# A two-layer attention and mixture-of-experts kernel on one core: where the second expert matrices of the first layer come from

## The chip, the cores and the metric

The kernel runs on one NeuronCore of a Trainium2 chip. The time is the device time of one execution in microseconds (us); the value given for a kernel is the median of several executions. The engines are PE (TensorE: matmul, and PEld for its weight loads), DVE (VectorE), ACT (ScalarE), POOL (GpSimd) and SP (SyncE, which here only issues DMAs). Each has its own instruction sequencer, written PEldq, SPq, ACTq and DVEq in the rows: the sequencer does the register and branch instructions and hands the rest on to its engine.

## What is computed

The program is two transformer layers on x of 8 x 256 x 256 floats (2048 tokens of width 256). Each layer is a cross attention with 16 heads and then a mixture of experts. The change is in the expert part of the first layer:

```python
logits = jnp.einsum('sbd,de->sbe', x, Wg) + bg + bias
vals, idx = jax.lax.top_k(logits, 2)
w = jax.nn.softmax(vals - jnp.max(vals, axis=-1, keepdims=True), axis=-1)
cw = jnp.einsum('sbk,sbke->sbe', w, jax.nn.one_hot(idx, 16, dtype=x.dtype))
h = jax.nn.relu(jnp.einsum('sbd,edh->esbh', x, W1) + b1[:, None, None, :])
y = jnp.einsum('esbh,ehd->esbd', h, W2) + b2[:, None, None, :]
out = jnp.einsum('esbd,sbe->sbd', y, cw)
```

There are 16 experts; W1 of one is 256 x 512 and W2 of one is 512 x 256, 512 KB each in float32. Only the two chosen experts of a token are computed. x is added to the result, and the second layer (attention on the same context, then 7 experts with a capacity and one shared expert) follows.

## The kernel before

The program is a row of blocks that each end with a barrier of all engines: attention 0, `route_block` (layer 0), `experts0_block`, attention 1, `route_block` (layer 1), `experts1_block`.

**Routing.** `route_block` makes normalized rows `hall`, which SP stores to the DRAM tensor `rows` in eight DMAs (L1260), and from them the logits, the two picks of each token, and `block_expert`: the (token, expert) pairs are sorted by expert and cut into NB0 = 47 blocks of 128 rows, each of one expert. In this block SP also loads b1 and b2 of all experts (L1256, L1257) and, behind the row stores, ten DMAs of what attention 1 needs (`ahead`: four matrices of 256 KB, two bias vectors, two broadcast rows, two parts of the context; L1264 to L1270). Then it waits until the rows are stored.

**Experts.** `experts0_block` runs over the 47 blocks: block 0 is begun ahead, a hardware loop (Fori) of ROUNDS = 11 rounds handles RING = 4 blocks in each, and LEFT = 3 blocks follow it unrolled. For block n:

- SP reads the expert's number from `block_expert` into a register (L1573), waits until the second matmuls of block n-4 are done (`y_made`), and loads W1 and W2 of that expert, 1024 KB, into one of four ring buffers `w` (L1575).
- POOL gathers the 128 rows of x by an indirect DMA (L1589).
- PE transposes x (`turn`, L1703), DVE copies the transpose to SBUF (L1668), PE does the first matmuls (`first`, L1713: 8 of them, 16 in the trace, each of 128 columns), ACT adds the bias and applies relu (L1608), PE does the second matmuls (`second`, L1722: 4, in the trace 8, of 256 columns) and DVE adds b2 (L1676), ACT stores 128 KB of result (L1616).

PE's order is first(n+1), turn(n+2), second(n). first(n+1) waits for `w_loaded` of its ring buffer and for the transposed x of block n+1 (`xT_ready`). second(n) waits for ACT's `hid_ready`. ACT and DVE already read the expert's number into a register for each block, to address b1 and b2 (L1603, L1672). PE addresses only fixed places.

Of the kernel before, what the change touches and what calls it, by code (L numbers as in the profile page):

```python
# [50 lines left out]
W0 = DC * F0 + FC0 * D  # L51
NB0 = (2 * T + E0 * (P - 1)) // P
ROWS0 = NB0 * P

# [1125 lines left out]
def route_block(nc, m, layer, E, a, hall, router, shared=None, biases=None, rows=None, W=None, ctxT=None, ahead=None):  # L1180
# [7 lines left out]
    with ctx:  # L1188
# [64 lines left out]
        def _(sp):  # L1253
            if biases:
                b1, b2, b_loaded = biases
                sp.dma_start(b1[:], a["b1"]).then_inc(b_loaded, 16)  # L1256
                sp.dma_start(b2[:].rearrange("p e d -> p (e d)"), a["b2"].rearrange("e d -> (e d)").partition_broadcast(P)).then_inc(b_loaded, 16)  # L1257
                for n in range(B):
                    sp.wait_ge(h_ready, n + 1)
                    sp.dma_start(rows[n * S:(n + 1) * S, :].rearrange("(t p) d -> p t d", p=P),  # L1260
                                 hall[:, n * TPB:(n + 1) * TPB]).then_inc(rows_stored, 16)
                loaded = ahead["loaded"]
                for name in ("Wk", "Wv", "Wq", "Wo"):
                    sp.dma_start(ahead[name.lower()][:], W[name].rearrange("(c p) n -> p c n", p=P)).then_inc(loaded, 16)  # L1264
                for w, name in enumerate(("bq", "bk")):
                    sp.dma_start(ahead["bias"][:, w], W[name].rearrange("(c p) -> p c", p=P), allow_slow_non_contiguous=True).then_inc(loaded, 16)
                for name in ("bo", "bv"):
                    sp.dma_start(ahead["bo" if name == "bo" else "bvb"][:], W[name].partition_broadcast(P)).then_inc(loaded, 16)
                for j in range(2):
                    sp.dma_start(ahead["cst"][:, j], ctxT.rearrange("(c p) t -> p c t", p=P)[:, :, j * S:(j + 1) * S]).then_inc(loaded, 16)  # L1270
                sp.wait_ge(rows_stored, 16 * B)
# [241 lines left out]
def experts0_block(nc, m, a, rows, ye, b1, b2, b_loaded):  # L1513

    ctx = ExitStack()
    with ctx:
# [48 lines left out]
        def w2(j, f):  # L1565
            return w[:, j, DC * F0 + f * D:DC * F0 + (f + 1) * D]

        @block.sync
        def _(sp):
            def load(i, j):  # L1570
# [4 lines left out]
                sp.dma_start(w[:, j], a["W_0"][bass.ds(e, 1)].rearrange("a p f -> p (a f)")).then_inc(w_loaded[j], 16)  # L1575

            with sp.Fori(0, ROUNDS) as i:
                for j in range(RING):
                    load(i, j)
            for j in range(LEFT):  # L1580
                load(ROUNDS, j)
# [110 lines left out]
        def _(pe):  # L1692
# [23 lines left out]
            def second(i, j):  # L1716
# [4 lines left out]
                for f in range(FC0):  # L1721
                    last = pe.matmul(ps[:, YB + j % 2, 0:D], hid[:, j % 2, f, :], w2(j, f), start=f == 0, stop=f == FC0 - 1)  # L1722
                last.then_inc(y_made, 1)

            def round_of(i, known):

                for j in range(min(known, RING)):
                    if j + 1 < known:
# [3 lines left out]
                    second(i, j)  # L1732
# [10 lines left out]
            first(0, 0)  # L1743
            with pe.Fori(0, ROUNDS) as i:
# [431 lines left out]
def two_layers(nc, a, out):  # L2176

    with ExitStack() as ctx:
# [17 lines left out]
        with ExitStack() as layer, signals(nc, m["resting"]) as signal:  # L2196
# [7 lines left out]
            with ExitStack() as experts, signals(nc, m["resting"]) as signal:  # L2204
                b_loaded = signal("b_loaded")
                b1, b2 = sb(experts, "b1", [P, E0, FC0]), sb(experts, "b2", [P, E0, D])
                with nc.sbuf_tensor("hall_0", [P, NT, D], F32) as hall:
                    route_block(nc, m, 0, E0, a, hall, routers[0], biases=(b1, b2, b_loaded), rows=rows0, W=W[1], ctxT=a["ctxT"], ahead=ahead)
                experts0_block(nc, m, a, rows0, ye0, b1, b2, b_loaded)
# [9 lines left out]
def lay_out(i):  # L2219
# [4 lines left out]
    def by_channel(w):  # L2224
# [13 lines left out]
        "W_0": c(np.concatenate([  # L2238
            i["L0_ffn_W1"].reshape(E0, DC, P, F0).transpose(0, 2, 1, 3).reshape(E0, P, DC * F0),
            i["L0_ffn_W2"].reshape(E0, FC0, P, D).transpose(0, 2, 1, 3).reshape(E0, P, FC0 * D)], axis=2)),  # L2240
# [23 lines left out]
```

## Time and profile before

| | |
|---|---|
| median of 3 runs | 1268.6 us (1268.25 to 1268.67) |
| span of the profiled execution (first to last instruction of the program) | 1262.1 us |
| PE busy | 1123.7 us, 89% |
| DVE, ACT, POOL busy | 55%, 47%, 29% |
| mean granted clock of PE | 0.955 |
| DMA traffic | 172.56 MB, mean 137 GB/s |
| the 47 blocks of experts of layer 0 | 278.80 to about 467 us of the span |
| loads of W1 and W2 there | 47 x 1024 KB |

The profile is one execution, seen by the hardware profiler. Its 1262.1 us are 6.5 us below the median, which holds start and end as well. A row of a timeline gives the start, the length, the engine, the line of the kernel, the operation and its operands, how many instructions were merged, and in brackets the idle time ahead of it and what ended that. The ends of matmuls are modelled: the length of a matmul reaches into the next, so a short stall may show as no idle time at all, and starts are to be compared with starts.

### The profile page before, as it was taken

To read this page: it belongs to the slowest core of one execution; us is meant where nothing else is said; L and a number is where in the kernel's file an instruction comes from. 1 tells how busy PE (TensorE), PEld (TensorE's weight loads), DVE (VectorE), ACT (ScalarE), POOL (GpSimd) and SP (SyncE) were. 2 spreads that over 40 slices of the span, in tenths; PEclk is the share of its full clock that TensorE was granted. 3 is DMA by queue.
4 is the path that set the end of the run, shared out by engine and by line. 5 is a ranking of instruction groups with operands and counts; after the bars stand their busy time and mean duration, and the time that the engine had idled before them with its cause. 6 is when DMAs were issued, how large, how long until landed. Compare 5 with 4: busy or idle time off the path is not lost. (4 is left out here: it accounts for less than half of the span.)

```text
span 1262.1 us, 25941 instructions
## 1 busy us (share of the span) xinstructions
PE 1123.7 (89%) x8539; PEld 974.6 (77%) x8539; DVE 690.8 (55%) x1558; ACT 595.9 (47%) x1211; POOL 360.7 (29%) x502
## 2 busy tenths in 40 slices
PE   5999998739999984888998679999999999999997
PEld 4788786329888873555665379999999999999996
DVE  4755666652222226676767655555556555555556
ACT  3566666313222222776787334444445444444432
POOL 6566650112222205776630145000000000000261
PEclk8899999859999996999999879999999999999999
DMA  7774461548999957568471221223232232232132
GB/s 182 175 180 120 129 179 37 193 159 292 332 330 325 314 207 163 111 136 146 89 125 24 100 89 59 79 63 112 72 103 76 87 109 87 86 100 73 50 97 80
DMA packets 88137, 172.56 MB, mean 137 GB/s; under 512 B 11251, under 2 KB 59949, under 8 KB 81792
## 3 DMA queue, kind: packets, MB, share of 16 engines
q1 hardware_dynamic: 71712, 136.15, 39.0%
q0 software_dynamic: 9584, 29.32, 7.9%
q10 hardware_dynamic: 6768, 6.16, 1.4%
q8 instruction: 40, 0.66, 0.2%
q14 instruction: 33, 0.27, 0.1%
HBM read 133.11 MB, written 39.20 MB: 137 GB/s over the span
## 5 line engine op out<-in xcount | busy, mean ns | idle before, releaser
L2136 PE MATMUL e_ps<-xT_e,wp_e 128*128 128x384 f32 (+1 forms) x1344 | 245.2, 331 | 4.0 <-DVE wp_e L2010 4.0
L2136 PEld LDWEIGHTS e_ps<-xT_e,wp_e 128*128 128x128 f32 x1344 | 221.7, 188 | 5.4 <-issue 4.1
L639 DVE TENSOR_REDUCE att_ps<-att_ps 128x2 f32<-128x512 f32 (+1 forms) x224 | 155.3, 697 | 103.5 <-PE att_ps L986 63.2
L1968 ACT ACTIVATE act_a_e<-e_ps 128x256 f32<-128x256 f32 (+2 forms) x176 | 77.8, 442 | 159.9 <-PE e_ps L2136 150.9
L2066 DVE TENSOR_TENSOR hid_e<-act_a_e,e_ps 128x256 f32<-128x256 f32 (+2 forms) x176 | 87.0, 494 | 116.6 <-ACT act_a_e L1968 102.4
L892 ACT ACTIVATE probs<-att_ps 128x384 f32<-128x384 f32 (+1 forms) x256 | 130.4, 546 | 41.4 <-PE att_ps L1018 29.0
L1972 ACT ACTIVATE hidp_e<-hid_e 128x256 fp32r<-128x256 f32 (+2 forms) x176 | 83.8, 476 | 127.3 <-DVE hid_e L2066 121.5
L2153 PE MATMUL e_ps<-wp_e,hidp_e 128*128 128x256 f32 (+1 forms) x1008 | 138.4, 282 | 2.9 <-DVE xres L2026 1.2
L2068 DVE TENSOR_TENSOR hidp_e<-hid_e,hidp_e 128x256 fp32r<-128x256 f32 (+2 forms) x176 | 87.8, 499 | 95.5 <-ACT hidp_e L1972 90.1
L2153 PEld LDWEIGHTS e_ps<-wp_e,hidp_e 128*128 128x128 f32 (+1 forms) x1008 | 130.7, 183 | 4.9 <-issue 4.1
L1608 ACT ACTIVATE hid_e<-e_ps,b_ahead 128x128 f32<-128x128 f32 x188 | 53.7, 368 | 139.9 <-PE e_ps L1713 129.2
L1919 POOL DMA_DIRECT2D done<-y_e x7 | 6.2, 893 | 384.3 <-DVE y_e L2050 384.3
L984 PE MATMUL att_ps<-ks,qs 96*128 96x256 bf16 (+1 forms) x512 | 102.4, 267 | 11.4 <-DMA qs<-parts 9.5
L2136 PE MATMUL e_ps<-xT_e,swp_e 128*128 128x256 f32 x768 | 106.0, 289 | 1.5 <-issue 0.8
L1016 PE MATMUL att_ps<-qs,ks 104*128 104x256 bf16 (+1 forms) x512 | 99.7, 262 | 3.4 <-ACT qs L882 1.5
L1713 PEld LDWEIGHTS e_ps<-xT_e,w_e 128*128 128x128 f32 x752 | 89.9, 194 | 16.5 <-issue 15.3
L2136 PEld LDWEIGHTS e_ps<-xT_e,swp_e 128*128 128x128 f32 x768 | 98.5, 195 | 2.8 <-DVE swp_e L2005 2.3
L1713 PE MATMUL e_ps<-xT_e,w_e 128*128 128x128 f32 x752 | 94.4, 279 | 6.4 <-DMA w_e<-in_W 5.8
L1589 POOL DMA_INDIRECT x_e<-rows,owner_e x47 | 44.7, 952 | 168.7 <-PE e_ps L1703 125.1
L882 ACT ACTIVATE qs<-att_ps 8x1024 bf16<-8x1024 f32 x64 | 65.1, 1017 | 52.9 <-PE att_ps L997 52.0
L1722 PE MATMUL e_ps<-w_e,hid_e 128*128 128x256 f32 x376 | 88.9, 380 | 0.0
L984 PEld LDWEIGHTS att_ps<-ks,qs 96*128 96x128 bf16 x512 | 48.0, 100 | 39.7 <-issue 20.7
(235 smaller groups left out, 1850.0 us busy)
## 6 DMA issues: line engine op xcount, KB each, us to landing
w_e<-in_W SPq DMA_DIRECT2D x47, 1024.0 KB
w_e<-in_W SPq DMA_DIRECT2D x57, 384.0 KB, 3.1
ks<-parts SPq DMA_DIRECT2D x96, 128.0 KB, 4.7
qs<-parts SPq DMA_DIRECT2D x96, 128.0 KB, 5.2
parts<-cut SPq DMA_DIRECT2D x30, 384.0 KB, 3.2
x_e<-rows SPq DMA_DIRECT2D x8, 768.0 KB, 5.6
done<-y_e ACTq DMA_DIRECT2D x47, 128.0 KB
rows<-zeros POOLq DMA_DIRECT2D x8, 736.5 KB, 6.6
```

The source lines that it names most:

```text
L639: dve.tensor_reduce(tops_at(at[3])[:, qt, x0:x0 + heads], src, AX.X, ALU.max).then_inc(reduced, 1)
L892: act.activation(probs[:, g % 2, x0, 0:WIDE], ps[:, TB + x0 % RING, 0:WIDE], ACT.Exp, scale=DK ** -0.5).then_inc(exped, 1)
L984: last = pe.matmul(out, qs[0:KS, j, hd, qt * P:(qt + 1) * P], ks[0:KS, j, hd, 0:keys(qt)], start=True, stop=not causal)
L1016: last = pe.matmul(out, ks[:, j, hd, kt * P:(kt + 1) * P], qs[:, j, hd, q0:S], start=True, stop=not causal)
L1713: last = pe.matmul(ps[:, HB + j % 2, f * P:(f + 1) * P], w1(j, c, f), xT[:, j % 2, c, :], start=c == 0, stop=c == DC - 1)
L1722: last = pe.matmul(ps[:, YB + j % 2, 0:D], hid[:, j % 2, f, :], w2(j, f), start=f == 0, stop=f == FC0 - 1)
L1968: act.activation(act_a[:, u % 2, 0:n], ps[:, AB + u % 2, 0:n], ACT.Silu).then_inc(silu_ready, 1)
L1972: act.activation(hidp[:, u % 2, 0, 0:n], hid[:, u % 2, 0:n], ACT.Copy).then_inc(hid_high, 1)
L2066: dve.tensor_tensor(hid[:, u % 2, 0:n], act_a[:, u % 2, 0:n], ps[:, BB + u % 2, 0:n], ALU.mult).then_inc(mixed, 1)
L2068: dve.tensor_tensor(hidp[:, u % 2, 1, 0:n], hid[:, u % 2, 0:n], hidp[:, u % 2, 0, 0:n].bitcast(F32), ALU.subtract).then_inc(hid_cut, 1)
L2136: last = pe.matmul(ps[:, bank + u % 2, 0:n], weights(lot, c, pw)[:, (b * DC + d) * P:(b * DC + d + 1) * P], xT[:, px, d, t0:t0 + n], start ...
L2153: last = pe.matmul(out, hidp[:, u % 2, px, t * P:t * P + rows], weights(lot, c, pw)[:, 2 * DC * P:], start=c == 0 and q == 0 and tile % 2 ...
```

## The change

W1 and W2 of the first layer's experts become two input tensors, `W1_0` (expert, partition, 1024 numbers) and `W2_0` (partition, expert, 1024 numbers). All of W2 (8 MB, 64 KB in each partition) is loaded in the routing block by four DMAs of 2 MB into the new tile `w2`, which stays until the experts of layer 0 are done. The ring buffers hold W1 alone, 512 KB. PE reads the number of the block's expert into a register and takes its second matmuls' moving operand from `w2` at that expert's place. PE waits once for all of W2, ahead of the loop. The ten DMAs for attention 1 move from SP's routing part to SP's experts part, between its loop and the last three loads of W1.

```diff
--- before.py
+++ after.py
@@ -48,8 +48,9 @@
 
 E0, F0 = 16, 512
 FC0 = F0 // P
-W0 = DC * F0 + FC0 * D
+W0 = DC * F0
 NB0 = (2 * T + E0 * (P - 1)) // P
+W2_LOADS = 4
 ROWS0 = NB0 * P
 
 E1, F1, CAP = 7, 1024, 732
@@ -1177,7 +1178,7 @@
                 project(B - 1, t)
 
 
-def route_block(nc, m, layer, E, a, hall, router, shared=None, biases=None, rows=None, W=None, ctxT=None, ahead=None):
+def route_block(nc, m, layer, E, a, hall, router, shared=None, biases=None, rows=None, w2=None):
 
 
 
@@ -1259,15 +1260,10 @@
                     sp.wait_ge(h_ready, n + 1)
                     sp.dma_start(rows[n * S:(n + 1) * S, :].rearrange("(t p) d -> p t d", p=P),
                                  hall[:, n * TPB:(n + 1) * TPB]).then_inc(rows_stored, 16)
-                loaded = ahead["loaded"]
-                for name in ("Wk", "Wv", "Wq", "Wo"):
-                    sp.dma_start(ahead[name.lower()][:], W[name].rearrange("(c p) n -> p c n", p=P)).then_inc(loaded, 16)
-                for w, name in enumerate(("bq", "bk")):
-                    sp.dma_start(ahead["bias"][:, w], W[name].rearrange("(c p) -> p c", p=P), allow_slow_non_contiguous=True).then_inc(loaded, 16)
-                for name in ("bo", "bv"):
-                    sp.dma_start(ahead["bo" if name == "bo" else "bvb"][:], W[name].partition_broadcast(P)).then_inc(loaded, 16)
-                for j in range(2):
-                    sp.dma_start(ahead["cst"][:, j], ctxT.rearrange("(c p) t -> p c t", p=P)[:, :, j * S:(j + 1) * S]).then_inc(loaded, 16)
+                w2_sb, w2_loaded = w2
+                for e in range(0, E0, E0 // W2_LOADS):
+                    some = slice(e, e + E0 // W2_LOADS)
+                    sp.dma_start(w2_sb[:, some], a["W2_0"][:, some]).then_inc(w2_loaded, 16)
                 sp.wait_ge(rows_stored, 16 * B)
             if shared:
                 sw, sw_loaded = shared
@@ -1510,7 +1506,7 @@
                 dve.tensor_copy(m["block_expert"][:], owner[:])
 
 
-def experts0_block(nc, m, a, rows, ye, b1, b2, b_loaded):
+def experts0_block(nc, m, a, rows, ye, b1, b2, b_loaded, w2_sb, w2_loaded, W, ahead):
 
     ctx = ExitStack()
     with ctx:
@@ -1562,8 +1558,8 @@
         def w1(j, c, f):
             return w[:, j, c * F0 + f * P:c * F0 + (f + 1) * P]
 
-        def w2(j, f):
-            return w[:, j, DC * F0 + f * D:DC * F0 + (f + 1) * D]
+        def w2(e, f):
+            return w2_sb[:, bass.ds(e, 1), f * D:(f + 1) * D].rearrange("p a d -> p (a d)")
 
         @block.sync
         def _(sp):
@@ -1572,11 +1568,20 @@
                 n = RING * i + j
                 e = sp.value_load(m["block_expert"][0:1, bass.ds(n, 1)], min_val=0, max_val=E0 - 1)
                 sp.wait_ge(y_made, free(n))
-                sp.dma_start(w[:, j], a["W_0"][bass.ds(e, 1)].rearrange("a p f -> p (a f)")).then_inc(w_loaded[j], 16)
+                sp.dma_start(w[:, j], a["W1_0"][bass.ds(e, 1)].rearrange("a p f -> p (a f)")).then_inc(w_loaded[j], 16)
 
             with sp.Fori(0, ROUNDS) as i:
                 for j in range(RING):
                     load(i, j)
+            loaded = ahead["loaded"]
+            for name in ("Wk", "Wv", "Wq", "Wo"):
+                sp.dma_start(ahead[name.lower()][:], W[name].rearrange("(c p) n -> p c n", p=P)).then_inc(loaded, 16)
+            for at_w, name in enumerate(("bq", "bk")):
+                sp.dma_start(ahead["bias"][:, at_w], W[name].rearrange("(c p) -> p c", p=P), allow_slow_non_contiguous=True).then_inc(loaded, 16)
+            for name in ("bo", "bv"):
+                sp.dma_start(ahead["bo" if name == "bo" else "bvb"][:], W[name].partition_broadcast(P)).then_inc(loaded, 16)
+            for j in range(2):
+                sp.dma_start(ahead["cst"][:, j], a["ctxT"].rearrange("(c p) t -> p c t", p=P)[:, :, j * S:(j + 1) * S]).then_inc(loaded, 16)
             for j in range(LEFT):
                 load(ROUNDS, j)
 
@@ -1713,23 +1718,27 @@
                         last = pe.matmul(ps[:, HB + j % 2, f * P:(f + 1) * P], w1(j, c, f), xT[:, j % 2, c, :], start=c == 0, stop=c == DC - 1)
                 last.then_inc(hid_made, 1)
 
-            def second(i, j):
+            def expert(i, j):
+                return pe.value_load(m["block_expert"][0:1, bass.ds(RING * i + j, 1)], min_val=0, max_val=E0 - 1)
+
+            def second(i, j, e):
                 n = RING * i + j
                 pe.wait_ge(hid_ready, ready(n, 2))
 
                 pe.wait_ge(y_ready, free(n))
                 for f in range(FC0):
-                    last = pe.matmul(ps[:, YB + j % 2, 0:D], hid[:, j % 2, f, :], w2(j, f), start=f == 0, stop=f == FC0 - 1)
+                    last = pe.matmul(ps[:, YB + j % 2, 0:D], hid[:, j % 2, f, :], w2(e, f), start=f == 0, stop=f == FC0 - 1)
                 last.then_inc(y_made, 1)
 
             def round_of(i, known):
 
                 for j in range(min(known, RING)):
+                    e = expert(i, j)
                     if j + 1 < known:
                         first(*at(i, j + 1))
                     if j + 2 < known:
                         turn(*at(i, j + 2))
-                    second(i, j)
+                    second(i, j, e)
 
             for k in range(2 * NT):
                 if k % MARKS == 0:
@@ -1741,6 +1750,7 @@
             turn(0, 0)
             turn(0, 1)
             first(0, 0)
+            pe.wait_ge(w2_loaded, 16 * W2_LOADS)
             with pe.Fori(0, ROUNDS) as i:
                 round_of(i, RING + 2)
             round_of(ROUNDS, LEFT)
@@ -2202,11 +2212,12 @@
                                 ("bo", [P, D]), ("bvb", [P, D]), ("cst", [P, 2, DC, S])):
                 ahead[name] = sb(layer, name, shape)
             with ExitStack() as experts, signals(nc, m["resting"]) as signal:
-                b_loaded = signal("b_loaded")
+                b_loaded, w2_loaded = signal("b_loaded"), signal("w2_loaded")
+                w2 = sb(experts, "w2", [P, E0, FC0 * D])
                 b1, b2 = sb(experts, "b1", [P, E0, FC0]), sb(experts, "b2", [P, E0, D])
                 with nc.sbuf_tensor("hall_0", [P, NT, D], F32) as hall:
-                    route_block(nc, m, 0, E0, a, hall, routers[0], biases=(b1, b2, b_loaded), rows=rows0, W=W[1], ctxT=a["ctxT"], ahead=ahead)
-                experts0_block(nc, m, a, rows0, ye0, b1, b2, b_loaded)
+                    route_block(nc, m, 0, E0, a, hall, routers[0], biases=(b1, b2, b_loaded), rows=rows0, w2=(w2, w2_loaded))
+                experts0_block(nc, m, a, rows0, ye0, b1, b2, b_loaded, w2, w2_loaded, W[1], ahead)
             with nc.sbuf_tensor("vals_1", [P, NT, H, DK], F32) as vals:
                 attend_block(nc, m, a, 1, W[1], parts[1], vals, (), a["ctxT"], ye=ye0, ahead=ahead, router=routers[1])
         with nc.sbuf_tensor("hall_1", [P, NT, D], F32) as hall:
@@ -2235,9 +2246,8 @@
         "bq_1": by_channel(i["L1_xattn_bq"]), "bk_1": by_channel(i["L1_xattn_bk"]), "bv_1": i["L1_xattn_bv"], "bo_1": i["L1_xattn_bo"],
         "Wg": i["L0_ffn_Wg"], "bg": i["L0_ffn_bg"], "bias": i["L0_ffn_bias"],
 
-        "W_0": c(np.concatenate([
-            i["L0_ffn_W1"].reshape(E0, DC, P, F0).transpose(0, 2, 1, 3).reshape(E0, P, DC * F0),
-            i["L0_ffn_W2"].reshape(E0, FC0, P, D).transpose(0, 2, 1, 3).reshape(E0, P, FC0 * D)], axis=2)),
+        "W1_0": i["L0_ffn_W1"].reshape(E0, DC, P, F0).transpose(0, 2, 1, 3).reshape(E0, P, W0),
+        "W2_0": i["L0_ffn_W2"].reshape(E0, FC0, P, D).transpose(2, 0, 1, 3).reshape(P, E0, FC0 * D),
         "b1": c(i["L0_ffn_b1"].reshape(E0, FC0, P).transpose(2, 0, 1)),
         "b2": i["L0_ffn_b2"],
         "ln_g": i["L1_ffn_ln_g"], "ln_b": i["L1_ffn_ln_b"], "Wr": i["L1_ffn_Wr"],
```

In SP's list the place behind the row stores is this before (`ahead` tiles are those of attention 1, b_ahead is b2, `waits` names semaphores):

```order
L1260 DMA rows<-hall 128x2x256 [waits h_ready_r0] x8
L1264 DMA wk_ahead<-in_Wk 128x2x256
L1264 DMA wv_ahead<-in_Wv 128x2x256
L1264 DMA wq_ahead<-in_Wq 128x2x256
L1264 DMA wo_ahead<-in_Wo 128x2x256
L1266 DMA bias_ahead<-in_bq 128x2x1
L1266 DMA bias_ahead<-in_bk 128x2x1
L1268 DMA bo_ahead<-in_bo 128x256
L1268 DMA bvb_ahead<-in_bv 128x256
L1270 DMA cst_ahead<-in_ctxT 128x2x256 x2
L1188 UNCONDITIONAL_BRANCH [waits rows_stored_r0]
```

and this after, where `w_ahead` is the new tile w2 and 128x4096 are four experts:

```order
L1261 DMA rows<-hall 128x2x256 [waits h_ready_r0] x8
L1266 DMA w_ahead<-in_W_0 128x4096 x4
L1189 UNCONDITIONAL_BRANCH [waits rows_stored_r0]
```

The ten DMAs stand now between the end of SP's loop and the load of block 44:

```order
L1571 DMA w_e<-in_W_0 128x1024
L1573 REGISTER_ALU
L1573 COMPARE_AND_BRANCH
L1578 DMA wk_ahead<-in_Wk 128x2x256
L1578 DMA wv_ahead<-in_Wv 128x2x256
L1578 DMA wq_ahead<-in_Wq 128x2x256
L1578 DMA wo_ahead<-in_Wo 128x2x256
L1580 DMA bias_ahead<-in_bq 128x2x1
L1580 DMA bias_ahead<-in_bk 128x2x1
L1582 DMA bo_ahead<-in_bo 128x256
L1582 DMA bvb_ahead<-in_bv 128x256
L1584 DMA cst_ahead<-in_ctxT 128x2x256 x2
L1569 TENSOR_LOAD block_expert
L1569 ISA x2
L1571 ISA [waits y_made_e0]
L1571 DMA w_e<-in_W_0 128x1024
```

So the last three loads of W1 have the ten in front of them, and the routing has only the four loads of W2 behind its row stores.

On PE one block of the loop is this before, from the wait for its weights to its second matmuls (REGISTER_ALU and ISA are the sequencer's):

```order
L1709 REGISTER_ALU [waits w_loaded2_e0]
L1713 MATMUL e_ps<-xT_e,w_e 128x128 [waits hid_ready_e0,xT_ready_e0]
L1713 MATMUL e_ps<-xT_e,w_e 128x128 x7
L1703 MATMUL e_ps<-ident,x_e 128x128 [waits xT_ready_e0,x_loaded3_e0]
L1703 MATMUL e_ps<-ident,x_e 128x128
L1722 MATMUL e_ps<-w_e,hid_e 128x256 [waits y_ready_e0,hid_ready_e0]
L1722 MATMUL e_ps<-w_e,hid_e 128x256 x3
```

and this after:

```order
L1722 ISA
L1722 TENSOR_LOAD block_expert
L1722 ISA x2
L1714 REGISTER_ALU [waits w_loaded2_e0]
L1718 MATMUL e_ps<-xT_e,w_e 128x128 [waits hid_ready_e0,xT_ready_e0]
L1718 MATMUL e_ps<-xT_e,w_e 128x128 x7
L1708 MATMUL e_ps<-ident,x_e 128x128 [waits xT_ready_e0,x_loaded3_e0]
L1708 MATMUL e_ps<-ident,x_e 128x128
L1730 ISA [waits y_ready_e0,hid_ready_e0]
L1730 MATMUL e_ps<-w_ahead,hid_e 128x256
L1730 ISA
L1730 MATMUL e_ps<-w_ahead,hid_e 128x256
```

(two more such pairs follow). PE's sequencer has a register load and three register instructions more ahead of each block's first matmuls, and one more ahead of each of the four second matmuls.

## Rows read from the trace of the kernel before

**Rows 1.** The page: PE's busy tenths and the DMA rate in 40 slices

```profile
PE   5999998739999984888998679999999999999997
...
GB/s 182 175 180 120 129 179 37 193 159 292 332 330 325 314 207 163 111 136 146 89 125 24 100 89 59 79 63 112 72 103 76 87 109 87 86 100 73 50 97 80
```

**Rows 2.** Busy time, granted clock, DMA share and rate in four stretches

```profile
core 0: us, PE busy (x) PEld busy (x) DVE busy (x) ACT busy (x) POOL busy (x), PEclk, DMA share, GB/s
...
233.00:237.00 4.00, 4.00 (x24) 2.19 (x24) 1.52 (x6) 2.31 (x5) 0.00 (x0) 0.97 0.89 254
237.00:245.00 8.00, 7.84 (x51) 4.05 (x50) 5.36 (x26) 3.79 (x8) 0.00 (x0) 1.00 1.10 374
...
262.00:274.00 12.00, 3.14 (x32) 2.43 (x32) 9.83 (x18) 2.48 (x4) 0.00 (x0) 0.50 0.81 309
...
300.00:461.00 161.00, 154.59 (x1042) 138.62 (x1041) 34.00 (x80) 45.74 (x160) 34.10 (x36) 1.00 0.94 321
```

**Rows 3.** Timeline of PE: start us, length us, operation, [idle <- what ended it]

```profile
278.80 4.80 PE L1713 MATMUL e_ps<-xT_e,w_e 128*128 128x128 f32 x32
...
285.38 1.95 PE L1713 MATMUL e_ps<-xT_e,w_e 128*128 128x128 f32 x16
...
292.84 1.95 PE L1713 MATMUL e_ps<-xT_e,w_e 128*128 128x128 f32 x16
...
294.85 1.89 PE L1722 MATMUL e_ps<-w_e,hid_e 128*128 128x256 f32 x8
296.57 1.95 PE L1713 MATMUL e_ps<-xT_e,w_e 128*128 128x128 f32 x16
...
304.84 2.02 PE L1713 MATMUL e_ps<-xT_e,w_e 128*128 128x128 f32 x16 [0.64 <-DMA w_e<-in_W]
...
461.37 1.95 PE L1713 MATMUL e_ps<-xT_e,w_e 128*128 128x128 f32 x16
```

**Rows 4.** Tile w_e from 285 to 467 us: what ended the engine's idle time

```profile
  DMA w_e<-in_W: 5.8, 13
```

**Rows 5.** The page's DMA issues: engine, count, size, median us to landing

```profile
w_e<-in_W SPq DMA_DIRECT2D x47, 1024.0 KB
w_e<-in_W SPq DMA_DIRECT2D x57, 384.0 KB, 3.1
...
done<-y_e ACTq DMA_DIRECT2D x47, 128.0 KB
```

**Rows 6.** PE's sequencer at the loop's end, 290 to 299 us: ns, first and last start

```profile
L1744 PEldq ALU_OP  x1: 32/32/32, 293.8 to 293.8; - x1
L1744 PEldq COMPARE_BRANCH  x1: 214/214/214, 293.9 to 293.9; - x1
```

**Rows 7.** Timeline of DVE, 294 to 296 us

```profile
295.13 0.42 DVE L1668 COPY xT_e<-e_ps 128x256 f32<-128x256 f32 x1 [1.56 <-PE e_ps L1703]
```

**Rows 8.** Sequencers of ACT and DVE in one block: the register load and its neighbours

```profile
L1603 ACTq FUSED_REGOPS  x2: 66/112/157, 292.2 to 292.6; - x2
...
L1603 ACTq SEQ_ASSERT  x1: 18/18/18, 292.8 to 292.8; - x1
...
L1672 DVEq FUSED_REGOPS  x2: 57/124/190, 291.4 to 292.2; - x2
...
L1672 DVEq SEQ_ASSERT  x1: 23/23/23, 292.4 to 292.4; - x1
```

**Rows 9.** Timeline of SP: DMA issues in routing, experts and attention 1

```profile
237.11 0.60 SPq L1264 DMA_DIRECT2D wk_ahead<-in_Wk  x1
...
243.10 0.95 SPq L1270 DMA_DIRECT2D cst_ahead<-in_ctxT  x2
262.98 4.17 SPq L1575 DMA_DIRECT2D w_e<-in_W  x4
...
293.17 4.09 SPq L1575 DMA_DIRECT2D w_e<-in_W  x2
...
495.94 0.40 SPq L413 DMA_DIRECT2D cst_ahead<-in_ctxT  x1
```

## The prediction

> **What bounds the kernel now.** Read the page's slices first, PE against GB/s [rows 1]. From the tenth slice to the fourteenth (284 to 442 us) the DMA engines move 292 to 332 GB/s, against 207 at most elsewhere, and PE shows nines: both are near their limit, and which of them sets the pace is to be found. The stretches say the same of 300 to 461 us: DMA share 0.94 at 321 GB/s, PE at its full granted clock (1.00, the level of 2.4 GHz) and busy 154.6 of 161 us [rows 2].
>
> Then read how far apart PE's blocks are, start to start. First matmuls of a block start at 292.84 and at 296.57, 3.73 us apart, and 285.38 to 292.84 is twice 3.73. Later 296.57 to 304.84 is 8.27 for two blocks, and the last of them waits 0.64 us for w_e [rows 3]. From block 2 (285.38) to block 46 (461.37) there are 44 steps in 175.99 us, 4.00 us each. At PE's own pace they would take 44 x 3.73 = 164.12 us, so **11.87 us** are lost in the stage. The idle time put down to the loads of w_e is only 5.8 us in 13 places [rows 4], but a matmul's modelled end reaches into the next, so that short stalls show none; the starts are to be trusted more.
>
> Is it the DMA that costs the 11.87? One block moves 1024 KB of weights, 128 KB stored by ACT [rows 5] and 128 gathered rows of 1 KB: 1.31 MB. At 321 GB/s [rows 2] that is 4.08 us, against 4.00 seen and 3.73 wanted. So the transfers are the slower chain by a little, and PE's own work is right behind. That caps what any cut in traffic can give.
>
> **What the change removes.** 47 loads of 1024 KB become 47 of 512 KB. A block now moves 0.79 MB, 2.45 us at the same 321 GB/s, a third below PE's 3.73. A load is issued 0.33 us into first(n-2) (292.84 in [rows 3], 293.17 in [rows 9]), and first(n) starts two steps after first(n-2), so it has 7.46 - 0.33 = 7.1 us. 384 KB land in 3.1 us [rows 5]; 512 KB at that rate take 4.1. PE's steps become 3.73 us: **-11.9 us**. What is late next is PE itself: its matmuls follow each other without a gap in a step of 3.73. I put nothing below that.
>
> **What it adds on PE.** Each block has a register load with three register instructions, and one register instruction ahead of each second matmul. No row shows a register load on PE, so its price comes from the other engines: on ACT the group runs from 292.2 to 292.8, 0.6 us, on DVE from 291.4 to 292.4, 1.0 us [rows 8]. The four of the second matmuls are of the kind FUSED_REGOPS, 57 to 190 ns [rows 8], so 0.2 to 0.8 us. I take 0.6 and 0.4; the ends together are 0.8 and 1.8.
>
> It costs nothing where the sequencer is ahead of the array. It is: at 293.8 it is at the loop's branch [rows 6], which in program order stands behind the second matmuls of that step, and those start only at 294.85 [rows 3]. The new load stands right there. From 293.8 the branch takes it to about 294.1, the load to 294.7 (at most 295.1). Behind it is the wait for the transposed rows, which DVE delivers at 295.13 + 0.42 = 295.55 [rows 7], and the array wants the next first matmuls at 296.57. So the cover is 1.4 us up to a wait that is there anyway, and 2.5 us until the array stands still. The other three blocks of a round have no branch. The four small ones stand among second matmuls that the sequencer hands over a microsecond early, and lie in the same cover. The single wait for W2 stands behind the first matmuls of block 0; queued behind it are those of block 1, which began within the 4.80 us from 278.80 [rows 3]. **0 us**, ends 0 and what the rival below gives.
>
> **What it adds in the routing.** SP's list has four loads of 2 MB instead of the ten. They begin at 237.1, as the first of the ten did [rows 9]. Loads from 237 to 245 us ran at 374 GB/s, those of weights from 262 to 274 at a mean of 309 with an idle part in it, and the slowest busy stretch here had 254 [rows 2]. 8.39 MB take 22.4 us at 374 and 33.0 at 254: W2 is there at 259.5 to 270.1. SP issues the first loads of W1 at 262.98 [rows 9]; four of 512 KB are 2.1 MB, 5.6 to 8.3 us. The latest case ends at 278.4, the usual one at 268.6, and PE wants block 0 at 278.80 [rows 3]. Before, 4.2 MB were issued at 262.98. SP's loads have no one waiting behind them: its next wait, for the row stores, is for DMAs ahead of them in the queue. **0 us**, ends -0.5 (the first gathers of x share the engines with less) and +1.
>
> One rule speaks against this load. The rows here showed no load slower than 254 GB/s. The Trainium skill, DMA: Bandwidth & Descriptors (section Latency and other measured facts), states that copies of 16 KiB per partition slow down when the pitch of the rows in HBM is a large power of two, to 207 GB/s at 512 KiB. W2_0 has exactly such pieces at a pitch of 64 KiB, below the least pitch that it lists; the loads of before had other pitches, and no run here shows the rule. At 207 GB/s the sum would have W2 in at 277.6 and block 0 of W1 some 2.5 us later, past 278.80.
>
> **What it moves.** The ten DMAs cost SP 243.10 + 0.95 - 237.11 = 6.9 us to issue in the routing, with the DMA engines full (share 1.10) [rows 2, 9]. A single one of the same kind costs 0.40 us in attention 1 [rows 9], ten of them 4.3 with gaps. In their new place they follow the load of block 43, issued 0.33 us into first(41). Counted from the start of first(41): 0.33 + 0.33 for that load, 0.3 for the loop's end, 4.3 to 6.9 for the ten, 0.6 for the register load, so block 44's load goes out at 5.9 to 8.5 us instead of 4.06, and lands 4.1 us later, at 10.0 to 12.6. PE wants it at three steps, 11.19. So the stall is 0 to 1.4 us, once; with a queue that is less than full I am nearer to the short issue times, and take **+0.5 us**. Blocks 45 and 46 follow with more room. Attention 1 has the data long before it begins, at about 467.
>
> **The sum.** -11.9 + 0 + 0 + 0.5 = -11.4 us. Against the profiled execution: 1262.1 - 11.4 = 1250.7. The 6.5 us around the span stay: 1268.6 - 11.4 = **1257.2 us**, -0.9%. Everything behind the stage starts earlier and is otherwise the same.
>
> **The rivals.**
> - **The register load empties PE's queue** (the slower side). If PE's array had to stand still while its sequencer reads SBUF, each block would gain 0.6 to 1.0 us of PE time. The price per block decides: from 11.4 / 46 = 0.25 us exposed it eats all the gain. With 0.6 us, 46 x 0.6 = 27.6, less 11.4: +16.2, 1285 us; with 1.0, 1303 us. For it: no row shows such a load on PE. Against: on ACT and DVE it runs beside their engines' work, and PE's sequencer is seen 1 us ahead [rows 6].
> - **The load is late only at the loop's end.** If PE needs longer after the branch with the longer body, up to 0.5 us in 11 rounds: +5, 1262 us. For it: cover is least there. Against: 1.4 us of cover.
> - **Only the idle time goes.** If the rest of the 11.87 is something other than weights (the gather, the stores, semaphores), 5.8 us go [rows 4] and 0.5 come: 1263 us. For it: the profile names no more. Against: 1.31 MB at 321 GB/s is the observed step. This is also the case in which the change doesn't do what it is meant to.
> - **W2 is late.** If its long pieces ran at half of the 374 GB/s seen, W2 would take 44.9 us, be in at 282.0, and W1 of block 0 behind it at 284.8: +6 us at block 0, with the gain 1263 us. It costs from the point where W2 and that load end after 278.80. For it: no load of this kernel had its layout. Against: 9 us of room at 374 GB/s. The rule of the Trainium skill's DMA page above is a case of this.
>
> **How the numbers follow.** Forecast 0.76; late only at the loop's end 0.04; only the idle time 0.06; W2 late 0.04; queue emptied 0.08, of which nearly all is slower; 0.02 for partial exposure that cancels the gain. The forecast's own range is 1254.5 to 1259.5: full gain with an easier entry and PE's clock granted a little earlier somewhere, against 1.4 us at block 44 and 1 us at the start. To hold 8 in 10 I reach up to the third rival, 1263. 0.2% is 2.5 us, about what a measurement of this kernel can tell from no change. Faster by more than that: 0.76 + 0.04 + 0.06 + 0.04 = 0.90; within: 0.02; slower: 0.08.
>
> **What would show it.** In the profile after: first matmuls of the blocks 3.73 us apart from first to last, with no idle time put down to w_e but perhaps once, at block 44; the DMA rate in the stage near 0.79 MB / 3.73 us = 211 GB/s; the register load on PE's sequencer ending ahead of DVE's copy of xT; W2 landed by 262 us; block 0 starting at 278.8 as before, and the routing as long as before. I am wrong if the steps are evenly longer than 3.73 (queue emptied), longer once in four (loop's end), or still 3.8 to 4.3 in an irregular row (not the weights).

## The result and the profile after

The changed kernel takes 1258.17 us (median of 6, 1256.49 to 1263.71), beside 1268.42 for the kernel before (median of 6). The ratio is 0.9916, 95% interval 0.9895 to 0.9938: faster by 0.84%, 10.25 us by the medians, 7.9 to 13.3 by the interval. The forecast was 1257.2.

The page of the kernel after, its PE and transfer slices:

```profile
span 1256.0 us, 26319 instructions
...
PE   6999999729999984898998679999999999999997
...
GB/s 181 176 179 126 122 175 49 246 239 183 209 215 207 213 142 172 124 131 127 98 126 9 101 93 52 82 64 113 85 90 80 93 102 86 87 106 68 50 98 80
```

The hump of 292 to 332 GB/s [rows 1] is gone: the same slices hold 183 to 215. In its place the two slices of the routing hold 246 and 239, where W2 is loaded now. The stretches of the kernel after (us; busy time and count of each engine; PE's granted clock, DMA share, GB/s):

```profile
core 0: us, PE busy (x) PEld busy (x) DVE busy (x) ACT busy (x) POOL busy (x), PEclk, DMA share, GB/s
237.00:245.00 8.00, 7.84 (x48) 4.04 (x47) 4.49 (x22) 3.84 (x8) 0.00 (x0) 1.00 1.07 394
245.00:262.00 17.00, 5.82 (x42) 3.16 (x41) 12.88 (x49) 3.21 (x6) 0.00 (x0) 0.75 1.00 422
...
300.00:450.00 150.00, 148.02 (x1028) 139.66 (x1028) 33.10 (x78) 44.72 (x157) 34.80 (x37) 0.99 0.74 219
```

Against [rows 2] the stage of the experts runs at 219 GB/s in place of 321, and W2 arrives at 394 to 422 GB/s. Now PE's timeline (start us, length us, operation, idle time and what ended it), first a stretch early in the loop, then the end of the stage:

```profile
291.79 1.95 PE L1718 MATMUL e_ps<-xT_e,w_e 128*128 128x128 f32 x16
...
295.52 1.95 PE L1718 MATMUL e_ps<-xT_e,w_e 128*128 128x128 f32 x16
...
299.25 1.95 PE L1718 MATMUL e_ps<-xT_e,w_e 128*128 128x128 f32 x16
...
441.06 1.95 PE L1718 MATMUL e_ps<-xT_e,w_e 128*128 128x128 f32 x16
...
446.93 2.68 PE L1718 MATMUL e_ps<-xT_e,w_e 128*128 128x128 f32 x16 [1.98 <-DMA w_e<-in_W]
449.40 0.63 PE L1708 MATMUL e_ps<-ident,x_e 128*128 128x128 f32 x2
449.82 2.73 PE L1730 MATMUL e_ps<-w_ahead,hid_e 128*128 x8
452.39 1.95 PE L1718 MATMUL e_ps<-xT_e,w_e 128*128 128x128 f32 x16
```

Where [rows 3] showed 3.73 at first and then 8.27 for two steps, with a wait for w_e, every step from block 2 to block 43 is 3.73 us. Two steps are not: block 43 to 44 takes 5.87 (446.93 - 441.06) and block 44 to 45 takes 5.46. The first has the only wait for w_e that is left. In the second nothing waits long, but its matmuls are slow: 0.63 us for two transposes in place of 0.38, 2.73 for the eight second matmuls in place of 1.89.

The profiled execution splits like this (us; the routing is counted from SP's first DMA in it, L1256 before and L1257 after):

| | before | after | difference |
|---|---|---|---|
| up to the routing | 228.2 | 229.2 | +1.0 |
| routing up to block 0 | 50.6 | 51.8 | +1.2 |
| block 0 to block 2 | 6.6 | 7.1 | +0.5 |
| block 2 to block 46 | 176.0 | 168.1 | -7.9 |
| block 46 to the end | 800.7 | 799.9 | -0.9 |
| span | 1262.1 | 1256.0 | -6.1 |

The first row is in code that did not change: over the ten profiled executions of this document it lies between 227.9 and 232.9 us. Executions of the kernel after spread over 7 us. The stage must be read by its steps, the total by the medians.

### The profile page after: what moved, and what is told of

Read it like the earlier page. It is cut to its first block and busy times, and to the rows that moved or that the text cites. A ratio compares the mean times of both kernels' runs of the same rounds, so it can differ in the third digit from the quotient of the medians.

```text
span 1256.0 us, 26319 instructions
## 1 busy us (share of the span) xinstructions
PE 1123.8 (89%) x8539; PEld 981.6 (78%) x8540; DVE 689.2 (55%) x1558; ACT 595.2 (47%) x1211; POOL 359.9 (29%) x502
## 5 line engine op out<-in xcount | busy, mean ns | idle before, releaser
L985 PE MATMUL att_ps<-ks,qs 96*128 96x256 bf16 (+1 forms) x512 | 101.7, 266 | 10.6 <-DMA qs<-parts 8.4
L1718 PEld LDWEIGHTS e_ps<-xT_e,w_e 128*128 128x128 f32 x752 | 93.3, 196 | 4.6 <-issue 2.3
L1730 PE MATMUL e_ps<-w_ahead,hid_e 128*128 x376 | 89.9, 382 | 0.0
```

The lines of the kernel that those rows point to most:

```text
L985: last = pe.matmul(out, qs[0:KS, j, hd, qt * P:(qt + 1) * P], ks[0:KS, j, hd, 0:keys(qt)], start=True, stop=not causal)
L1718: last = pe.matmul(ps[:, HB + j % 2, f * P:(f + 1) * P], w1(j, c, f), xT[:, j % 2, c, :], start=c == 0, stop=c == DC - 1)
```

## The experiments

Eight kernels ran beside the kernel before. All are judged by two things: the steps of PE's blocks, which repeat to 0.01 us where nothing waits, and the time. Each trace is of one execution; the time is a median of 4 to 10, beside 16 or 17 of the kernel before.

**Theory.** The traffic of a block sets the step before; with half the weights gone PE's own 3.73 us do. The register load on PE lies in its sequencer's lead. The two long steps at the end come from the ten DMAs that were moved in front of the last three loads. **Rivals.** Only the waits that the profile names (5.8 us) are the weights' part; the register load costs the array time; the long steps are chance or something else.

### Where the ten DMAs stand

ahead_last, the changed kernel with them behind the last loads:

```diff
+            for j in range(LEFT):
+                load(ROUNDS, j)
             loaded = ahead["loaded"]
...
                 sp.dma_start(ahead["cst"][:, j], a["ctxT"].rearrange("(c p) t -> p c t", p=P)[:, :, j * S:(j + 1) * S]).then_inc(loaded, 16)
-            for j in range(LEFT):
-                load(ROUNDS, j)
```

> The changed kernel with one move: the ten DMAs for attention 1 stand behind the last three loads of W1, not ahead of them. Theory (the tail): in the changed kernel's profile the steps to blocks 45 and 44 take 5.47 and 5.87 us in place of 3.73, because block 44's W1 lands 2.0 us late behind the ten, and PE's clock then falls to half for one stretch. Then all steps from block 2 to 46 are 3.73 here (164.2 us in all, 168.07 in the changed kernel) and the time is 3.9 us shorter, 1254.3. Rival (the clock's fall was coming anyway, and the last blocks wait for something else, the gathers or the stores): one or both long steps stay, and at most 2.1 us go, 1256 to 1258.

Measured: 1254.57 us, ratio 0.9888 (0.9857 to 0.9920); all 44 steps are 3.73 us, 164.19 in sum. PE's timeline at the end of the stage, where the long steps were:

```profile
445.08 1.95 PE L1718 MATMUL e_ps<-xT_e,w_e 128*128 128x128 f32 x16
...
448.81 1.95 PE L1718 MATMUL e_ps<-xT_e,w_e 128*128 128x128 f32 x16
...
452.55 1.95 PE L1718 MATMUL e_ps<-xT_e,w_e 128*128 128x128 f32 x16
```

These are blocks 44, 45 and 46, a step of 3.73 each. So both long steps came from the order in SP's list, the slow one too: with no stall, no fall of the clock followed.

after_again is the changed kernel without an edit, run again:

> The changed kernel as it is, beside the others on one chip. 1258.2, the two long steps at the end (blocks 44 and 45) again: their cause is an order in SP's list, not chance. If they were chance, they would be gone or elsewhere in this execution. Against ahead_last the difference should be the 3.9 us of those steps.

Measured: 1258.98 us, ratio 0.9915 (0.9892 to 0.9937). The steps are the same to 0.06 us, 5.93 and 5.46 at the same two blocks. Here is PE's timeline at the first of them:

```profile
441.16 1.95 PE L1718 MATMUL e_ps<-xT_e,w_e 128*128 128x128 f32 x16
...
447.09 2.83 PE L1718 MATMUL e_ps<-xT_e,w_e 128*128 128x128 f32 x16 [2.04 <-DMA w_e<-in_W]
```

The two long steps are not chance. The time of ahead_last was taken in an earlier set of runs, but regs3 below, which is ahead_last with more register loads, ran in the same set as after_again: 1254.75, 4.2 us below it. The 3.9 us of the steps are shown by the traces; the times agree with them, but their intervals (0.9861 to 0.9906 and 0.9892 to 0.9937 of before) still touch.

ahead_routing puts the ten back into the routing, behind the loads of W2:

```diff
                     sp.dma_start(w2_sb[:, some], a["W2_0"][:, some]).then_inc(w2_loaded, 16)
+                loaded = ahead["loaded"]
+                for name in ("Wk", "Wv", "Wq", "Wo"):
+                    sp.dma_start(ahead[name.lower()][:], W[name].rearrange("(c p) n -> p c n", p=P)).then_inc(loaded, 16)
...
```

> The changed kernel with the ten DMAs back in the routing, behind the four loads of W2. Theory (the tail): same steps of 3.73 us to the end, 1254.3; W2 lands as before (24.4 us after its first issue at the latest), the ten behind it by about 268, the first loads of W1 after them still ahead of block 0. So the move of the ten bought nothing. Rival (the routing has no room for both): block 0 of W1 or the first gathers come late and block 0 starts 1 us or more later than the 280.96 of the changed kernel, 1255.5 or more.

Measured: 1254.93 us, ratio 0.9894 (0.9865 to 0.9922). All 44 steps are 3.73, as in ahead_last. But the rival has its part too: from the routing's first DMA to block 0 it takes 52.9 us, against 51.8 and 51.6 in the two executions of the changed kernel. SP's timeline in the routing shows why:

```profile
244.76 1.20 SPq L1269 DMA_DIRECT2D wq_ahead<-in_Wq  x1
246.01 9.86 SPq L1269 DMA_DIRECT2D wo_ahead<-in_Wo  x1
255.91 8.48 SPq L1271 DMA_DIRECT2D bias_ahead<-in_bq  x1
264.44 0.56 SPq L1271 DMA_DIRECT2D bias_ahead<-in_bk  x1
```

In the kernel before, the issues of Wo and of the first bias took 0.93 and 0.52 us; here they take 9.86 and 8.48: behind four loads of 2 MB and three of 256 KB SP is held at the issue itself. It is issuing DMAs until 267.53, while DVE has done its last work of the routing at 266.62. DVE then stands idle for 1.99 us at the barrier, against 0.87 in the changed kernel: SP is the late one, by 1.1 us. It issues the first load of W1 at 269.21, 37.1 us after the routing's first DMA, where the changed kernel has 36.0. The difference in time to ahead_last is within the noise.

before_ahead_tail is the kernel before with only the ten DMAs moved to where the change puts them:

```diff
-                loaded = ahead["loaded"]
-                for name in ("Wk", "Wv", "Wq", "Wo"):
...
             with sp.Fori(0, ROUNDS) as i:
                 for j in range(RING):
                     load(i, j)
+            loaded = ahead["loaded"]
+            for name in ("Wk", "Wv", "Wq", "Wo"):
...
             for j in range(LEFT):
                 load(ROUNDS, j)
```

> The kernel before with one part of the change alone: the ten DMAs for attention 1 moved from the routing to SP's list between its loop and the last three loads, which here carry 1024 KB each. Theory (bytes in front of a load that PE is close behind): 1.8 MB more go through a stage that is bound by its transfers, 5.6 us at 321 GB/s, and the wait is long enough for PE's clock to fall as in the changed kernel: two long steps at blocks 44 and 45, in sum 5 to 8 us, 1274 to 1277. Rival (the last loads have room, since block 44 to 46 are the end): under 2 us, 1270.

Measured: 1276.84 us, ratio 1.0048 (1.0019 to 1.0077), 7.3 us slower than before by the medians, 2.4 to 9.8 by the interval. The steps to blocks 44 and 45 are 9.30 and 6.55 us. PE's timeline at block 44:

```profile
466.06 3.75 PE L1713 MATMUL e_ps<-xT_e,w_e 128*128 128x128 f32 x16 [5.32 <-DMA w_e<-in_W]
469.60 0.64 PE L1703 MATMUL e_ps<-ident,x_e 128*128 128x128 f32 x2
470.03 2.74 PE L1722 MATMUL e_ps<-w_e,hid_e 128*128 128x256 f32 x8
```

The move alone is a loss, larger where the loads behind it are larger: 8.4 us above two steps of 3.73, against 3.9 in the changed kernel. Both parts are there again, the stall (5.32) and the slow matmuls after it.

### Whether bytes set the step

before_w1_only is the kernel before with its loads cut to W1. It leaves out the right W2, so its output is not that of the function; the work on PE is the same:

```diff
+            for j in range(RING):
+                sp.dma_start(w[:, j, DC * F0:], a["W_0"][j][:, DC * F0:]).then_inc(w2_once, 16)
...
-                sp.dma_start(w[:, j], a["W_0"][bass.ds(e, 1)].rearrange("a p f -> p (a f)")).then_inc(w_loaded[j], 16)
+                sp.dma_start(w[:, j, 0:DC * F0], a["W_0"][bass.ds(e, 1)].rearrange("a p f -> p (a f)")[:, 0:DC * F0]).then_inc(w_loaded[j], 16)
```

> The kernel before, whose 47 loads take W1 alone; W2 of experts 0 to 3 is loaded once into the four ring buffers and used for every block (the second matmuls then use other experts' weights; their work is the same). No register load on PE, no W2 in the routing. Theory (traffic is the cause of the 4.00 us steps): steps of 3.73 from block 2 to 46, 164.2 us against 175.99, and the time is 11.8 us below before, 1256.6. Rival (only the waits that the profile names are the weights' part, 5.8 us; the rest is gathers, stores or semaphores): steps of 3.86 on average, 1262.6.

Measured: 1254.00 us, ratio 0.9885 (0.9852 to 0.9917). All 44 steps are 3.73, 164.19 us in sum. So the cut in traffic alone, without register loads and without W2 in the routing, gives the whole 11.8 us of the stage; the rival's 5.8 is out. The time falls by more, 15.1 us by the medians; the part on the prediction comes back to that.

traffic_twice is ahead_last with the bytes put back:

```diff
-                sp.dma_start(w[:, j], a["W1_0"][bass.ds(e, 1)].rearrange("a p f -> p (a f)")).then_inc(w_loaded[j], 16)
+                for half in range(2):
+                    sp.dma_start(w[:, j, half], a["W1_0"][bass.ds(e, 1)].rearrange("a p f -> p (a f)")).then_inc(w_loaded[j], 16)
```

> ahead_last with each block's W1 loaded twice, once to its place and once to a buffer that nobody reads; PE waits for both. W2 stays resident, PE keeps its register loads. A block moves 1.31 MB again. Theory (bytes per block set the step): steps of 4.0 us on average again, 176 us for 44 of them, irregular, DMA share over 0.9 at about 320 GB/s, and the time is 11.8 us above ahead_last, 1266. Rival (the size of the pieces or W2's place in the ring made the steps long, not bytes): steps stay near 3.73, below 1257.

Measured: 1264.59 us, ratio 0.9969 (0.9942 to 0.9996), 10.0 us above ahead_last. The steps are irregular again, 3.73 to 5.89, 173.8 us in sum, 9.6 above 164.2. One stretch of each, ahead_last and then traffic_twice (columns as above):

```profile
300.00:440.00 140.00, 140.00 (x980) 132.34 (x979) 31.79 (x76) 42.60 (x150) 35.03 (x37) 1.00 0.71 209
```

```profile
300.00:440.00 140.00, 135.27 (x919) 123.24 (x918) 30.15 (x71) 41.15 (x144) 34.08 (x36) 1.00 0.97 328
```

With the same code on PE, twice the weight bytes take the DMA share from 0.71 to 0.97 and open gaps on PE. In traffic_twice the profile puts only this much idle time down to the loads (tile w_e, 290 to 466 us):

```profile
  issue: 12.2, 19
  DMA w_e<-in_W: 5.5, 9
```

5.5 us, where the steps lose 9.6: PE's idle time undercounts, as it did before [rows 4]. (The row of issue is all PEld's, the weight loads; PE has no other idle time here.)

### How long the register load may be

The load on PE's sequencer in the changed kernel (kind, count, ns least/median/most, first and last start):

```profile
L1722 PEldq FUSED_REGOPS  x80: 42/151/165, 281.4 to 457.2; - x80
L1722 PEldq TENSOR_LOAD <-block_expert x47: 298/302/502, 280.9 to 456.8; - x47
L1722 PEldq SEQ_ASSERT  x47: 18/18/28, 281.6 to 457.4; - x47
```

302 ns; with its register instructions the group behind one loop's branch runs from 297.0 to 297.6. To see whether it is hidden or free, it was repeated in ahead_last:

```diff
                 for j in range(min(known, RING)):
-                    e = expert(i, j)
+                    for _ in range(3):
+                        e = expert(i, j)
```

> ahead_last with the register load on PE done three times for each block (two of the three serve nothing). In the changed kernel a group of load and register instructions takes PE's sequencer 0.75 us (297.00 to 297.75), and at the loop's end the array takes the next first matmuls 1.5 us after the group's end, in the other blocks 2 us after. Theory (the load runs beside the array, in the sequencer's lead): two more groups, 1.5 us, fit: steps of 3.73 but perhaps 0.1 to 0.3 more once in four; the time is that of ahead_last within 3 us. Rival (PE's array waits for a register load, for a part of it that the profile does not show): every step is longer by 0.6 us or more, 47 of them 28 us or more: 1283.

Measured: 1254.75 us, ratio 0.9883 (0.9861 to 0.9906). Three of four steps are 3.73; the one behind the loop's branch is 3.76 to 3.83. The 44 steps take 164.72, 0.52 more than with one load. The same with six loads:

> The same with six loads: five more groups, 3.75 us. Theory (a lead that can be used up): the lead of about 2.0 us is exceeded by some 1.75 us in each block, by 2.2 at the loop's end: steps of 5.5 to 6.0, and 47 x 1.9 = 89 us more than ahead_last, 1343 us, more where PE's clock falls. Rival (the sequencer is limited by something else and the loads are free): no change.

Measured: 1331.36 us, ratio 1.0477 (1.0451 to 1.0503). Steps are 5.2 us and, behind the branch, 5.9; 237.4 us in sum, 73.2 more than ahead_last. PE's timeline of regs6, and below it the six register loads of one block on the sequencer:

```profile
304.12 2.02 PE L1718 MATMUL e_ps<-xT_e,w_e 128*128 128x128 f32 x16 [1.27 <-issue]
...
310.06 3.56 PE L1718 MATMUL e_ps<-xT_e,w_e 128*128 128x128 f32 x16 [1.97 <-issue]
...
316.05 2.02 PE L1718 MATMUL e_ps<-xT_e,w_e 128*128 128x128 f32 x16 [0.36 <-issue]
```

```profile
L1722 PEldq TENSOR_LOAD <-block_expert x6: 296/300/381, 300.0 to 303.3; - x6
```

The idle time has "issue" as its cause: PE waits for nothing else that the profile shows, so I put it to its own sequencer. The lead is real and finite. The six loads start 0.66 us apart (300.0 to 303.3), so a group more costs 0.66 us, not the 0.75 of my expectations. Two more, 1.3 us, fit but for 0.05 us behind the branch. Five more, 3.3 us, exceed the lead by 1.5 us a step and by 2.1 behind the branch, which leaves a lead of about 1.8 and 1.2 us for anything beyond the one load. My expectation for regs6 was 89 us; 76.8 came, by the medians of regs6 and ahead_last. The prediction's rival of +16 to +34 us, an array that stands still in every register load, is refuted by regs3.

## Why the prediction was right, point by point

**What bounds the stage: right.** The step before is set by bytes. Taking them away gives 3.73 (before_w1_only), putting them back gives 3.95 on average (traffic_twice). Reading the starts and not the idle time was the choice that mattered: 11.8 us were to be had in the execution that I read, not 5.8.

**The removed traffic, -11.9 us: right.** 175.99 became 164.19 in ahead_last, ahead_routing and before_w1_only, the kernels without the tail stall: -11.80. The stage's DMA rate is 219 GB/s, near the 211 of my sign.

**The register load on PE, 0 us: right.** The group takes 0.6 us, as I took it, and is covered. The cover, too, is nearly as I said. The sequencer and the copy of the transposed x in the changed kernel:

```profile
L1754 PEldq ALU_OP  x1: 32/32/32, 296.4 to 296.4; - x1
L1722 PEldq TENSOR_LOAD <-block_expert x1: 306/306/306, 297.0 to 297.0; - x1
297.81 0.42 DVE L1673 COPY xT_e<-e_ps 128x256 f32<-128x256 f32 x1 [1.56 <-PE e_ps L1708]
```

The sequencer is at the loop's branch (L1754) at 296.4, and the array takes the next first matmuls at 299.25, 2.8 us later; before, the same two points were 293.8 [rows 6] and 296.57 [rows 3], 2.8 us as well. So the four small register instructions among the second matmuls cost the lead nothing that shows. The branch with its neighbours took 0.6 us to the load, where I had 0.3. The group ends at 297.6, ahead of DVE's copy at 298.23 and 1.6 us ahead of the array.

**W2 in the routing: right in its own terms.** I had it landed between 259.5 and 270.1. The four loads (ns per issue, then us to landing):

```profile
L1266 SPq DMA_DIRECT2D w_ahead<-in_W x4: 462/580/711, 238.1 to 239.8; - x4
...
DMA to landing us min/median/max: 11.5/17.9/24.4
```

Even the last landed by 264.2 (my sign of being right said 262). The rate was 422 GB/s at full share, so W2's 64 KiB pitch cost nothing that shows. I had misread the figure that I held against it. The row of the Trainium skill (DMA: Bandwidth & Descriptors, Latency and other measured facts) on row pitches is about copies between two tensors in HBM, and the 207 GB/s at its least pitch, 512 KiB, stand there beside 214 as the full rate. So it was not the price of a slow load that I took it for, and no run here has a pitch of its table.

**The entry, 0 us with ends -0.5 and +1: just above its end, cause open.** From the routing's first DMA to block 0 took 50.2 to 50.6 us in the three kernels without W2 in the routing and 50.8 to 52.0 in the six with it that leave the ten DMAs out of it; 51.8 in the changed kernel's profile, 1.2 above before. There PE was slower even before W2's first load is issued at 238.1. The stretch from 229 to 237 us, the kernel before and then after (columns as above):

```profile
229.00:237.00 8.00, 7.50 (x35) 3.77 (x36) 5.52 (x18) 4.23 (x9) 2.26 (x9) 0.79 0.93 291
```

```profile
229.00:237.00 8.00, 6.57 (x22) 3.15 (x22) 6.24 (x19) 3.69 (x7) 2.24 (x9) 0.57 0.84 252
```

The mean granted clock is 0.79 there and 0.57, so PE was at 1.2 GHz for 3.5 us more, and did 22 matmuls in place of 35 (it also got there 1 us later). W2's bytes were not under way yet. The other traces say the same: in the 8 us from each kernel's own first DMA of the routing, the granted clock is 0.79 in all three kernels without W2 there and 0.57 to 0.68 in all seven with it, and the two of the seven with the highest clock, 0.68 and 0.64, have the shortest entries, 50.8 and 51.1 us. So the longer entry goes with PE's clock ahead of W2's loads, and not with their bytes. What in these kernels lowers the clock at that point is not shown. The 0.5 us more from block 0 to block 2 are no mark of W2: outside regs6 this stretch takes 6.5 to 8.2 us, and 7.9 in before_w1_only, which loads no W2 in the routing.

**The moved DMAs, +0.5 us: this is the term that was mis-sized.** It measured 168.07 - 164.19 = 3.9 us. SP's timeline at the end of the changed kernel's stage:

```profile
434.48 0.40 SPq L1578 DMA_DIRECT2D wk_ahead<-in_Wk  x1
...
439.33 0.95 SPq L1584 DMA_DIRECT2D cst_ahead<-in_ctxT  x2
441.06 4.41 SPq L1571 DMA_DIRECT2D w_e<-in_W  x3
```

The ten were issued in 5.8 us, inside my 4.3 to 6.9, and block 44's load went out 7.5 us into first(41), inside 5.9 to 8.5. Two things were not in the sum. First, I gave the load 4.1 us to land; in ahead_last, where nothing stands ahead of them, loads of this size take 4.0 at the median, so the figure was right for such a queue. Here it took 5.7 (441.06 to the sequencer's next step at 446.7), because the bytes of the ten were still ahead of it. The stretches say so (columns as above):

```profile
441.00:445.00 4.00, 3.95 (x28) 3.37 (x26) 0.85 (x2) 1.14 (x4) 0.00 (x0) 1.00 1.11 346
445.00:448.00 3.00, 1.07 (x9) 1.10 (x10) 0.42 (x1) 0.00 (x0) 0.00 (x0) 1.00 1.03 395
448.00:452.00 4.00, 4.00 (x18) 3.59 (x17) 0.42 (x1) 1.14 (x4) 0.00 (x0) 0.57 0.26 98
```

That made the stall 2.1 us, above my upper end of 1.4. Second, the stall has a price of its own: after 3 us in which PE was busy for 1.07, its granted clock is 0.57 over the next four, that is, at 1.2 GHz for most of them, and the block in work loses another 1.7 us. I had noted the clock at 1.00 through the whole stage and never asked what one stall would do to it; the stalls of the kernel before, 0.8 us at most, had not touched it.

A stall of this length does not always bring the fall, and what decides is open. traffic_twice has one of 1.99 us, and PE's clock stays at 1.00 behind it (its timeline, then the stretch):

```profile
424.48 2.02 PE L1719 MATMUL e_ps<-xT_e,w_e 128*128 128x128 f32 x16 [1.99 <-DMA w_e<-in_W]
```

```profile
424.50:428.50 4.00, 3.96 (x27) 3.41 (x27) 0.42 (x1) 1.14 (x4) 0.95 (x1) 1.00 1.02 395
```

regs6 has ten stalls of 1.89 to 1.97 us, one behind each branch: after four of them the granted clock of the next 4 us is 0.57 to 0.65, after six it is 1.00. The stalls at the tail, 1.98, 2.04 and 5.32 us, were all three followed by a fall.

**Why the total came so close: two errors that cancel.** The forecast of 1257.2 lies 1 us from the median all the same, and that is luck. The tail was 3.4 us too small in the sum. The gain was too small as well: without the long steps the medians lie 14.5 (ahead_last), 14.2 (ahead_routing) and 15.1 us (before_w1_only) below the kernel before, where the steps give 11.8. The likely reason is the one execution of before that I read. In every other listed run the device time is 1.8 to 1.9 us above the span, so this span of 1262.1 belongs to a time of about 1264 (an estimate), some 4.7 us below the median; the 6.5 us between them are not all start and end. And the irregular loop of before does not take the same time twice. before_ahead_tail has the same code up to block 43. Its first matmuls of blocks 2 and 43:

```profile
288.49 1.95 PE L1713 MATMUL e_ps<-xT_e,w_e 128*128 128x128 f32 x16
...
456.76 2.02 PE L1713 MATMUL e_ps<-xT_e,w_e 128*128 128x128 f32 x16 [0.19 <-DMA w_e<-in_W]
```

These 41 steps took 168.27 us, in the profile of before 164.19, and at 3.73 they would take 153.0. So the loads cost 15.3 us in one execution and 11.2 in the other. What they cost on average no trace shows, but a gain of about 14 us less a tail of 3.9 is what the medians of the changed kernel have, 10.25 and 10.6.

**The better version.** ahead_last is the change with the ten DMAs behind the last loads: 0.9888 (0.9857 to 0.9920) of before, 1254.6 us. Against the changed kernel it saves the 3.9 us of the two long steps; the three kernels without these steps and with W2 resident have medians of 1254.57, 1254.93 and 1254.75, the two sets of the changed kernel 1258.17 and 1258.98.

## What to carry to other kernels

Compare starts of equal pieces of work across a loop before trusting the idle time of PE: here the idle time named about half of the loss, in two kernels. Where such steps are irregular, read more than one execution: the same loop lost 11.2 us in one and 15.3 in another. A cut in traffic is worth what separates the transfers' time per step from the engine's own, and no more; 512 KB less per block was worth 0.27 us of 4.00 in the execution read. And when a DMA is moved to make room elsewhere, count its bytes in front of the next load that someone is waiting for, not only its issue time, and give a possible fall of PE's clock a term of its own where a stall of 2 us is to be expected: it came behind some of them here and added 1.7 us.

## What the runs showed of the hardware that I had not expected

- An issue on SP can itself be held: with four loads of 2 MB and three of 256 KB ahead, one DMA issue took 9.86 us and the next 8.48, where the others of that list take 0.4 to 1.2. SP was then 1.1 us late at the barrier.
- One stall of 2.0 us on PE was followed by 3.4 us at half clock in the changed kernel, in both executions with a profile; it nearly doubled the stall's price. A stall of 1.99 us in traffic_twice, and six of ten such stalls in regs6, were followed by full clock.
- PE's sequencer runs 2.8 us ahead of the array at the loop's branch, and four register instructions of 46 ns among the second matmuls did not change that. A register load of 0.3 us, 0.66 with its register instructions when repeated, is free up to a lead that can be used up: two more cost 0.05 us behind the branch, five more 1.5 to 2.1 us in every step.
- Four loads with pieces of 16 KB and a pitch of 64 KB ran at 422 GB/s over 17 us. In the 8 us from 237 to 245, where the row stores run too, it was 394, against 374 with the ten smaller loads before.
